# State space layers: the product with the gate behind the scan of its slot, TensorE's output product one slot later

## The chip, the cores and the metric

The kernel runs on one core of a Trainium2 chip. The metric is the device time of one execution in microseconds. A core has five engines that run side by side, each through its own instructions in their order: PE (TensorE, matrix products, with its weight loads shown as PEld), DVE (VectorE), ACT (ScalarE), POOL (GpSimd) and SP, which here only issues DMAs. They wait for one another through semaphores: a wait stops its engine, and with it all that is queued behind the wait.

## The reference, cut to what matters

The program is a chain of blocks over a batch of 8 sequences of 256 tokens with 128 features. The change lies in the second attention place, which holds four state space (Mamba) layers:

```python
for i in range(N_LAYERS):                       # 4
    xn = _layernorm(x, ln_w[i], ln_b[i])
    x = _mamba(xn, ...) + x
# _mamba
xz = einsum('bsd,ed->bse', x, in_w); x_in, z = split(xz)
xc = silu(conv(x_in) + cb)                      # 256 inner features, 4 taps
dbl = einsum('bsd,ed->bse', xc, xp_w)           # 8 for dt, 16 rows B, 16 rows C
dt = softplus(einsum(dtr, dt_w) + dt_b)
h = h * exp(dt * A) + (dt * xc) * B             # over time, 256 features x 16 states
y = sum over states of h * C
y = (y + xc * Dp) * silu(z)                     # the product with the gate
return einsum('bse,de->bsd', y, out_w)          # the output product
```

## The kernel before, in words

The 256 inner features lie as two halves (c) on 128 partitions, time along the row. A *unit* is one sequence of one layer: 4 layers x 8 sequences = 32 units, numbered 0 to 31 in this text (unit u = s + 8 l). A unit has NP = 8 *slots*, and a slot handles two of the 16 states, so that its tiles are 128 x (2 states x 2 halves x 256 steps) = 128 x 1024. `over_units` runs the slots of all units in order; per layer it writes out sequence 0, rolls sequences 1 to 4 in a loop of two pairs, and writes out 5 to 7. Each engine has its own `slot` function, called for the same slots in the same order; what it issues there is its order in the program, and semaphores couple the engines.

In slot i of a unit:
- ACT: the decays exp(dt A) of the pair i + 1 into one of two halves of a bank group (L1332, four instructions). They may start when the scan that read this half is done (`h_ready`).
- DVE: `input_term`, the product of step size, input and B for the pair i + 1 (`mam_dbu`, L1193), except for pairs 3 and 6, which POOL makes (L1267); then the scan of pair i along time (L1215), which writes `mam_state`.
- POOL: the product of the state of pair i - 1 with the rows C (`mam_state_c`, L1257), behind that pair's scan.
- PE: the sum over states, an identity matmul of `mam_state_c` of pair i - 2 that accumulates in the unit's bank (L1426, four passes for a pair). So the sum of a unit's last two pairs falls in slots 0 and 1 of the next unit.

The end of a unit lies in the next one (`last`): DVE multiplies the finished sum by the gate (`mam_y_gated`, L1200), which waits for the sum of pair 7; PE adds the residual and multiplies by the output weights (the output product, L1438 to L1444, and L1441 in the last layer alone, a second residual), which waits for `yg_ready`; ACT copies the result out of the bank in slot 4 (L1356).

Between these the engines prepare the next unit (`nxt`) and the one behind it (`after`): PE the rows for B, C and dt (L1375, L1381) in slots 0 and 1, ACT the parts of softplus in slots 1 to 3, PE their sum in slot 4 (`step_sizes`, L1411 to L1414), DVE the step sizes `mam_dt` from it, in slot 4 behind scan 4 (L1185), POOL the product of step size and input in slot 5 (L1245). The layer norm of the unit after next is taken by DVE in slot 2 (L1175, L1178), by POOL in slot 3 and by ACT and PE in slots 4 and 5; its convolution in slots 6 and 7.

No scheduler is involved: the order on each engine is the order of these functions.

Of the kernel before, what the change touches and what calls it, by code (L numbers as in the profile page):

```python
# [11 lines left out]
ALU = mybir.AluOpType  # L12
# [4 lines left out]
B, S = 8, 256  # L17
# [1068 lines left out]
def state_space_layers(K, tag, m):  # L1086
# [4 lines left out]
    NP = NS // 2  # L1091
    BY_POOL = (3, 6)
    flat = lambda a: a.rearrange("p c t -> p (c t)")
# [3 lines left out]
    y_bank = lambda q: K.ps[4 + q]  # L1097
    scratch = nc.dram_tensor(f"{tag}_bc_rows", (2 * NS, S), F32, kind="Internal").ap()
    with ExitStack() as scope:
# [12 lines left out]
        def over_units(eng, slot, tail):  # L1112
            at = lambda l, s, q: (l, s, q) if s < B else (l + 1, s - B, q) if l + 1 < L else None

            def main(l, s, q, last):
                for i in range(NP):
                    slot(i, (l, s, q), last, at(l, s + 1, 1 - q) if isinstance(s, int) else (l, s + 1, 1 - q),
                         at(l, s + 2, q) if isinstance(s, int) else (l, s + 2, q))
            for l in range(L):
                main(l, 0, 0, (l - 1, B - 1, 1) if l > 0 else None)  # L1120
                with eng.Fori(0, 2) as pair:
                    for d in (1, 2):
                        main(l, pair * 2 + d, d % 2, (l, pair * 2 + (d - 1), 1 - d % 2))
                for s in range(5, B):
                    main(l, s, s % 2, (l, s - 1, 1 - s % 2))
            for i in range(tail):
                slot(i, None, (L - 1, B - 1, 1), None, None)
# [16 lines left out]
        with nc.Block() as block:  # L1144
            @block.sync
            def _(sp):
                for u in range(L * B):
                    sp.wait_ge(rows_ready, u + 1)
                    if u:
                        for k in range(4):  # L1150
                            sp.wait_ge(loaded[k], u * 16)
                    sp.dma_start(scratch, rows[0:2 * NS, :]).then_inc(rows_out, 16)
                    sp.wait_ge(rows_out, u * 16 + 16)
                    for k in range(4):
                        if u:
                            sp.wait_ge(hc_ready, u * NP - NP + 2 * k + 2)
                        src = scratch.rearrange("(k r) t -> k (r t)", k=4)[k:k + 1, :].broadcast_to([P, 8 * S])
                        sp.dma_start(spread[:, k, :, :], src).then_inc(loaded[k], 16)

            @block.vector  # L1160
            def _(dve):
                dve.sem_inc(h_ready, 2)

                def prepare(i, nxt, after):
                    if after and i == 2:
                        l, s, q = after
                        a = s + l * B
                        xs = lambda t: xm[:, bass.ds(s * W + t * P, P)]
                        link = chain(dve, dve_s)
                        if nxt:  # L1170
                            dve.wait_ge(bias_ready, a)
                        if l > 0:
                            dve.wait_ge(done, a - B + 3)
                        for t in range(TS):
                            k = dve.bn_stats(N.bn[:, t, :], xs(t))  # L1175
                        link(k)
                        for t in range(TS):
                            k = dve.bn_aggr(N.mv[:, t, :], N.bn[:, t, :])  # L1178
                        k.then_inc(N.stats, 1)
                    if nxt and i == 4:  # L1180
                        l, s, q = nxt
                        b = s + l * B
                        dve.wait_ge(dt_sum, b + 1)
                        dve.wait_ge(relu_ready, b + 1)
                        dve.tensor_tensor(flat(dt[:, q, :, :]), K.ps[7][:, :], flat(vw[:, :, :]), ALU.add).then_inc(dt_ready, 1)  # L1185

                def input_term(u, j):
                    if j not in BY_POOL:
                        dve.wait_ge(loaded[j // 2], u * 16 + 16)
                        if not (isinstance(u, int) and u * NP + j < 4):  # L1190
                            dve.wait_ge(h_ready, u * NP + j - 1)
                        dve.wait_ge(dup_ready, u + 1)
                        dve.tensor_tensor(dbu[:, j % 4, :, :, :], both(K.ps[6][:, :].rearrange("p (c t) -> p c t", c=C)),  # L1193
                                          b_rows(j), ALU.mult).then_inc(dbu_dve, 1)

                def slot(i, now, last, nxt, after):
                    if last and i == 2:
                        l, s, q = last
                        dve.wait_ge(sum_done, (s + l * B) * NP + NP)
                        dve.tensor_tensor(flat(yg[:, :, :]), y_bank(q)[:, :], flat(zs[:, q, :, :]),  # L1200
                                          ALU.mult).then_inc(yg_ready, 1)
                    if now:
                        l, s, q = now
                        u = s + l * B
                        g = u * NP + i
                        if i + 1 < NP:
                            input_term(u, i + 1)
                        if i in BY_POOL:
                            dve.wait_ge(dbu_pool, pool_count(u, i))
                        else:  # L1210
                            dve.wait_ge(dbu_dve, dve_count(u, i))
                        if not (isinstance(u, int) and g < 4):
                            dve.wait_ge(hc_ready, g - 3)
                        dve.wait_ge(da_ready, g + 1)
                        dve.tensor_tensor_scan(flat2(h[:, i % 4, :, :, :]), decay(i), flat2(dbu[:, i % 4, :, :, :]), 0.0,  # L1215
                                               ALU.mult, ALU.add).then_inc(h_ready, 1)
                        if nxt and i + 1 == NP:
                            input_term(u + 1, 0)
                    prepare(i, nxt, after)

                before_units(prepare)
                input_term(0, 0)
                over_units(dve, slot, 3)

            @block.gpsimd
# [141 lines left out]
            def _(pe):  # L1367
# [48 lines left out]
                def slot(i, now, last, nxt, after):  # L1416
                    prepare(i, nxt, after)
                    at = lagged(i, 2, NP, now, last)
                    if at:
                        l, s, q, j = at  # L1420
                        u = s + l * B
                        if j == 0:
                            pe.wait_ge(z_ready, u + 1)
                        pe.wait_ge(hc_ready, u * NP + j + 1)
                        for n in range(2):
                            k = pe.matmul(y_bank(q)[:, :], K.ident[:, :], flat(hc[:, j % 4, n, :, :]),  # L1426
                                          start=(j == 0 and n == 0), stop=(j == NP - 1 and n == 1))
                        k.then_inc(sum_done, 1)
                        if j == 0:
                            for c in range(C):  # L1430
                                pe.matmul(y_bank(q)[:, c * S:(c + 1) * S], skip[:, l, c, :], xc[:, q, c, :],
                                          start=False, stop=False)
                    step_sizes(i, nxt)
                    if last and i == 2:
                        l, s, q = last
                        pe.wait_ge(yg_ready, s + l * B + 1)
                        for t in range(TS):
                            pe.matmul(y_bank(q)[:, t * P:(t + 1) * P], K.ident[:, :],  # L1438
                                      xm[:, bass.ds(s * W + t * P, P)], start=True, stop=False)
                            if l + 1 == L:  # L1440
                                pe.matmul(y_bank(q)[:, t * P:(t + 1) * P], K.ident[:, :],  # L1441
                                          K.x[:, bass.ds(s * W + t * P, P)], start=False, stop=False)
                            for c in range(C):
                                k = pe.matmul(y_bank(q)[:, t * P:(t + 1) * P], yg[:, c, t * P:(t + 1) * P],  # L1444
                                              f(l, "outw")[:, c * P:(c + 1) * P], start=False, stop=(c == C - 1))
                        k.then_inc(out_ps, 1)
# [3 lines left out]
                    step_sizes(i, nxt)  # L1450

                before_units(prepare_all)
                over_units(pe, slot, 3)

# [1325 lines left out]
```

## Time and profile before

| | |
|---|---|
| median of 3 runs | 2816.95 us (2815.59 to 2816.97) |
| the profiled execution | 2811.49 us, span 2809.6 us |
| mean granted TensorE clock | 0.961 of full speed |
| PE busy | 2484.8 us, 88% |
| DVE busy | 1942.2 us, 69% |
| ACT busy | 1700.1 us, 61% |
| POOL busy | 1144.5 us, 41% |

The span is the time from the first to the last instruction on the core. The shares are means over the whole program. POOL is busy 9 tenths and more of each slice only in the state space stage, from about 560 to 1434 us. There the costliest groups of the page are L1257 on POOL (256 instructions of 2360 ns), L1215 on DVE (256 of 2277 ns) and L1426 on PE (1024 passes). The page's chain of what ended last names only instructions of the last block, so it says nothing on this stage; its waits and timelines do. "Idle before" in square brackets is the time that an engine stood still ahead of an instruction, and behind the arrow is what released it. Where DVE instructions follow one another directly, a row begins some 0.08 us before the row above it ends.

### The profile page before, as it was taken

How to read it: one execution, taken by the hardware profiler on the slowest of the kernel's cores; microseconds unless marked ns; L12 is line 12 of the kernel's file. 1: busy time of each engine (PE TensorE's matmuls, PEld its weight loads, DVE VectorE, ACT ScalarE, POOL GpSimd, SP SyncE). 2: the span in 40 equal slices, each digit the busy share in tenths (PEclk: the TensorE clock that was granted, in tenths of full speed). 3: DMA queues.
4: the chain of work that ended last, by engine and by line, in shares of the span. 5: the costliest groups of instructions: out<-in, count | busy, mean ns of one | idle time of the engine just before them, and what ended most of it. 6: DMA issues, size and time to landing. Idle time of an engine off the chain costs nothing. (4 is left out here: it accounts for less than half of the span.)

```text
span 2809.6 us, 38135 instructions
## 1 busy us (share of the span) xinstructions
PE 2484.8 (88%) x11190; PEld 1409.4 (50%) x11190; DVE 1942.2 (69%) x3923; ACT 1700.1 (61%) x3566; POOL 1144.5 (41%) x919
## 2 busy tenths in 40 slices
PE   7999978499999999999978899978869998799977
PEld 4766634245555555555433344345544444555555
DVE  6888755499999999999955444356644444577754
ACT  3555522399999999999923244357754443466644
POOL 1000010299999999999930000042210001254432
PEclk9999989799999999999989999979999998999998
DMA  2000033134444444344433112000002110000000
GB/s 103 1 1 1 1 99 76 61 136 164 153 151 158 159 163 153 151 160 158 158 125 82 55 61 99 22 1 1 0 1 106 61 61 26 1 1 0 0 0 16
DMA packets 34612, 205.55 MB, mean 73 GB/s; under 512 B 4000, under 2 KB 5152, under 8 KB 13216
## 3 DMA queue, kind: packets, MB, share of 16 engines
q1 hardware_dynamic: 34464, 203.83, 20.1%
q8 instruction: 62, 1.02, 0.1%
q14 instruction: 86, 0.70, 0.1%
HBM read 201.19 MB, written 2.62 MB: 73 GB/s over the span
## 5 line engine op out<-in xcount | busy, mean ns | idle before, releaser
L1257 POOL TENSOR_TENSOR mam_state_c<-mam_state,weights_r 128x1024 f32<-128x1024 f32 x256 | 601.3, 2360 | 38.2 <-DVE mam_state L1215 37.0
L1215 DVE TENSOR_TENSOR_SCAN mam_state<-banks,mam_dbu 128x1024 f32<-128x1024 f32 x256 | 580.2, 2277 | 0.6 <-ACT banks L1332 0.6
L1426 PE MATMUL banks<-mam_state_c,identity 128*128 128x512 f32 x1024 | 479.6, 606 | 8.9 <-POOL mam_state_c L1257 8.9
L1332 ACT ACTIVATE banks<-mam_dt,mam_a_neg 128x255 f32<-128x255 f32 x1024 | 425.1, 461 | 31.9 <-DVE mam_state L1215 31.1
L1426 PEld LDWEIGHTS banks<-mam_state_c,identity 128*128 128x128 f32 x1024 | 185.4, 191 | 215.0 <-issue 181.7
L1193 DVE TENSOR_TENSOR mam_dbu<-banks,weights_r 128x1024 f32<-128x1024 f32 x192 | 227.8, 1200 | 6.8 <-ACT banks L1340 6.8
L424 ACT ACTIVATE at_probs<-banks,at_nmax 128x256 f32<-128x256 f32 x256 | 117.7, 472 | 137.8 <-DVE at_nmax L365 137.8
L2392 POOL TENSOR_TENSOR at_attention<-at_relu 128x512 f32<-128x512 f32 x128 | 131.0, 1041 | 124.4 <-ACT at_relu L2436 83.3
L896 DVE TENSOR_TENSOR m2a_hidden<-m2a_gelu,m2a_comb_spread 128x512 f32<-128x512 f32 x120 | 80.8, 690 | 116.3 <-ACT m2a_gelu L923 113.8
L896 DVE TENSOR_TENSOR m2b_hidden<-m2b_gelu,m2b_comb_spread 128x512 f32<-128x512 f32 x120 | 80.7, 690 | 116.4 <-ACT m2b_gelu L923 113.8
L1267 POOL TENSOR_TENSOR mam_dbu<-mam_dt_u,weights_r 128x1024 f32<-128x1024 f32 x64 | 151.0, 2359 | 0.0
L923 ACT ACTIVATE m2a_gelu<-banks,weights_r 128x512 f32<-128x512 f32 x128 | 85.2, 685 | 101.9 <-PE banks L943 101.8
L923 ACT ACTIVATE m2b_gelu<-banks,weights_r 128x512 f32<-128x512 f32 x128 | 85.2, 685 | 101.7 <-PE banks L943 101.7
L1762 ACT ACTIVATE at_probs<-at_scores,at_negated_max 128x160 f32<-128x160 f32 x256 | 95.0, 421 | 58.7 <-DVE at_negated_max L1601 56.0
L976 PE MATMUL banks<-m2a_hidden,weights_r 128*128 128x512 f32 x256 | 121.3, 597 | 2.2 <-DVE m2a_hidden L896 2.2
L976 PE MATMUL banks<-m2b_hidden,weights_r 128*128 128x512 f32 x256 | 121.3, 597 | 2.2 <-DVE m2b_hidden L896 2.2
L943 PE MATMUL banks<-m2a_xnt,weights_r 128*128 128x512 f32 x256 | 122.6, 602 | 0.0
L943 PE MATMUL banks<-m2b_xnt,weights_r 128*128 128x512 f32 x256 | 122.4, 601 | 0.0
L144 POOL TENSOR_SCALAR at_ln_rs<-at_ln_mv 128x2 f32<-128x2 f32 x16 | 4.4, 274 | 280.9 <-DVE at_ln_mv L346 252.2
L1400 PE MATMUL banks<-mam_xn_padded,weights_r 128*128 128x256 f32 x512 | 117.9, 383 | 0.7 <-ACT mam_xn_padded L1312 0.7
L1400 PEld LDWEIGHTS banks<-mam_xn_padded,weights_r 128*128 128x128 f32 x512 | 98.1, 192 | 28.2 <-issue 14.4
L365 DVE TENSOR_REDUCE at_nmax<-banks 128x2 f32<-128x512 f32 x128 | 82.3, 684 | 38.6 <-PE banks L468 34.5
(525 smaller groups left out, 5115.2 us busy)
## 6 DMA issues: line engine op xcount, KB each, us to landing
weights_r<-mam_bc_rows SPq DMA_DIRECT2D x128, 1024.0 KB, 4.6
m2a_comb_spread<-m2a_comb_rows SPq DMA_DIRECT2D x15, 1024.0 KB, 7.6
m2b_comb_spread<-m2b_comb_rows SPq DMA_DIRECT2D x15, 1024.0 KB, 8.2
m1a_comb_spread<-m1a_comb_rows SPq DMA_DIRECT2D x14, 512.0 KB, 7.4
m1b_comb_spread<-m1b_comb_rows SPq DMA_DIRECT2D x14, 512.0 KB, 7.1
weights_r<-in_mb SPq DMA_DIRECT2D x1, 4332.0 KB, 12.9
weights_r<-in_m SPq DMA_DIRECT2D x1, 4200.0 KB, 13.0
weights_r<-in_a SPq DMA_DIRECT2D x1, 2632.0 KB, 12.7
```

The lines of the kernel that those rows point to most:

```text
L896: dve.tensor_tensor(hid[:, g % 3, c, :], gelu[:, g % 2, c, :], weights, ALU.mult).then_inc(hid_ready, 1)
L923: act.activation(gelu[:, g % 2, c, :], h_bank(g, c)[:, :], ACT.Gelu, bias=b1[:, 2 * e + c:2 * e + c + 1]).then_inc(gelu_ready, 1)
L943: pe.matmul(h_bank(g, c)[:, :], w1[:, e * 256 + c * P:e * 256 + (c + 1) * P], R.xnt[:, p % 2, :], start=True, stop=True).then_inc(h_ps, 1)
L976: i = pe.matmul(y[:, :], w2[:, (2 * e + c) * P:(2 * e + c + 1) * P], hid[:, g % 3, c, :], start=False, stop=(e == E - 1 and c == 1))
L1193: dve.tensor_tensor(dbu[:, j % 4, :, :, :], both(K.ps[6][:, :].rearrange("p (c t) -> p c t", c=C)), b_rows(j), ALU.mult).then_inc(dbu_dve, 1)
L1215: dve.tensor_tensor_scan(flat2(h[:, i % 4, :, :, :]), decay(i), flat2(dbu[:, i % 4, :, :, :]), 0.0, ALU.mult, ALU.add).then_inc(h_ready, 1)
L1257: pool.tensor_tensor(hc[:, j % 4, :, :, :], h[:, j % 4, :, :, :], c_rows(j), ALU.mult).then_inc(hc_ready, 1)
L1267: pool.tensor_tensor(dbu[:, (i + 2) % 4, :, :, :], both(du[:, q, :, :]), b_rows(i + 2), ALU.mult).then_inc(dbu_pool, 1)
L1332: i = act.activation(decay(j)[:, o + 1:o + S], dt[:, q, c, 1:S], ACT.Exp, scale=aneg[:, l, k:k + 1])
L1400: k = pe.matmul(K.ps[7][:, c * S:(c + 1) * S], f(l, "taps")[:, t * 256 + c * P:t * 256 + (c + 1) * P], xpad[:, q, t:t + S], start=(t == 0) ...
L1426: k = pe.matmul(y_bank(q)[:, :], K.ident[:, :], flat(hc[:, j % 4, n, :, :]), start=(j == 0 and n == 0), stop=(j == NP - 1 and n == 1))
L2392: pool.tensor_tensor(at[:, i % 4, :, :], rel[:, i % 4, :, :], rel[:, i % 4, :, :], ALU.mult).then_inc(at_ready, 1)
```

## The change

On DVE, in the slot with i == 2, the product of the unit before with its gate is issued behind the scan of the slot and no longer ahead of it. On PE, the output product of the unit before is issued in slot 3, behind the sum over pair 1, and no longer in slot 2, behind the sum over pair 0. The tail of PE's slots behind the last unit is one slot longer for that.

```diff
 def slot(i, now, last, nxt, after):          # DVE
-    if last and i == 2:
-        l, s, q = last
-        dve.wait_ge(sum_done, (s + l * B) * NP + NP)
-        dve.tensor_tensor(flat(yg[:, :, :]), y_bank(q)[:, :], flat(zs[:, q, :, :]),
-                          ALU.mult).then_inc(yg_ready, 1)
     if now:
...
         if nxt and i + 1 == NP:
             input_term(u + 1, 0)
+    if last and i == 2:
+        l, s, q = last
+        dve.wait_ge(sum_done, (s + l * B) * NP + NP)
+        dve.tensor_tensor(flat(yg[:, :, :]), y_bank(q)[:, :], flat(zs[:, q, :, :]),
+                          ALU.mult).then_inc(yg_ready, 1)
     prepare(i, nxt, after)
...
     step_sizes(i, nxt)                       # PE
-    if last and i == 2:
+    if last and i == 3:
         l, s, q = last
         pe.wait_ge(yg_ready, s + l * B + 1)
...
-over_units(pe, slot, 3)
+over_units(pe, slot, 4)
```

PE's order before, in a unit outside the rolled loop, from the sum over pair 7 of the unit before and pair 0 (the first row, `x4`) to the step sizes of slot 4:

```order
L1426 MATMUL banks<-mam_state_c,identity 128x512 x4
L1431 MATMUL banks<-mam_conv,mam_skip_diagonal 128x256 x2
L1438 MATMUL banks<-mam_xm,identity 128x128
L1444 MATMUL banks<-weights_r,mam_y_gated 128x128 x2
L1438 MATMUL banks<-mam_xm,identity 128x128
L1444 MATMUL banks<-weights_r,mam_y_gated 128x128 x2
L1426 MATMUL banks<-mam_state_c,identity 128x512 x4
L1411 MATMUL banks<-mam_dt_exp,identity 128x512
L1412 MATMUL banks<-mam_dt_abs,identity 128x512
L1414 MATMUL banks<-mam_dt_ln,identity 128x512
```

The same place now:

```order
L1426 MATMUL banks<-mam_state_c,identity 128x512 x4
L1431 MATMUL banks<-mam_conv,mam_skip_diagonal 128x256 x2
L1426 MATMUL banks<-mam_state_c,identity 128x512 x2
L1438 MATMUL banks<-mam_xm,identity 128x128
L1444 MATMUL banks<-weights_r,mam_y_gated 128x128 x2
L1438 MATMUL banks<-mam_xm,identity 128x128
L1444 MATMUL banks<-weights_r,mam_y_gated 128x128 x2
L1426 MATMUL banks<-mam_state_c,identity 128x512 x2
L1411 MATMUL banks<-mam_dt_exp,identity 128x512
L1412 MATMUL banks<-mam_dt_abs,identity 128x512
L1414 MATMUL banks<-mam_dt_ln,identity 128x512
```

The output product stood ahead of the sums over pairs 1 and 2, and stands between them now.

DVE's order before in the same unit, from the input term of slot 1 to scan 2:

```order
L1193 TENSOR_TENSOR mam_dbu<-banks,weights_r 128x1024
L1211 REGISTER_ALU
L1213 REGISTER_ALU
L1214 REGISTER_ALU
L1215 SCALAR_TENSOR_TENSOR mam_state<-banks,mam_dbu 128x1024
L1200 TENSOR_TENSOR mam_y_gated<-banks,mam_gate 128x512
L1211 REGISTER_ALU
L1214 REGISTER_ALU
L1215 SCALAR_TENSOR_TENSOR mam_state<-banks,mam_dbu 128x1024
```

And now (L1206 to L1210 are the lines 1211 to 1215 of before, L1217 is the line 1200):

```order
L1193 TENSOR_TENSOR mam_dbu<-banks,weights_r 128x1024
L1206 REGISTER_ALU
L1208 REGISTER_ALU
L1209 REGISTER_ALU
L1210 SCALAR_TENSOR_TENSOR mam_state<-banks,mam_dbu 128x1024
L1206 REGISTER_ALU
L1209 REGISTER_ALU
L1210 SCALAR_TENSOR_TENSOR mam_state<-banks,mam_dbu 128x1024
L1217 TENSOR_TENSOR mam_y_gated<-banks,mam_gate 128x512
```

The gate product went from between scans 1 and 2 to behind scan 2. The orders of ACT, POOL and SP are the same in both kernels.

## Rows read from the trace of the kernel before

**Rows 1.** Busy time by stretch: first unit, units 1 to 9, the last layer's periods.

```profile
core 0: us, PE busy (x) PEld busy (x) DVE busy (x) ACT busy (x) POOL busy (x), PEclk, DMA share, GB/s
562.46:589.40 26.94, 22.97 (x60) 12.09 (x60) 25.57 (x20) 23.98 (x49) 24.11 (x15) 0.83 0.28 102
589.40:832.53 243.13, 232.75 (x757) 125.91 (x756) 235.49 (x181) 229.04 (x459) 232.76 (x136) 1.00 0.43 158
1237.81:1401.77 163.96, 155.76 (x515) 84.51 (x514) 156.98 (x118) 151.33 (x302) 154.96 (x87) 1.00 0.41 158
```

**Rows 2.** Waits of the state space stage: who waited for whom, us in total, times, longest.

```profile
POOL mam_state_c L1257 <- DVE mam_state L1215: 37.0, 33, 10.9
DVE mam_y_gated L1200 <- PE banks L1426: 29.6, 31, 5.2
DVE mam_dt L1185 <- PE banks L1414: 3.3, 7, 1.3
```

**Rows 3.** Timeline of DVE, unit 14: start us, us, engine line op, tiles, count [idle before].

```profile
947.00 0.69 DVE L1200 TENSOR_TENSOR mam_y_gated<-banks,mam_gate 128x512 f32<-128x512 f32 x1 [0.81 <-PE banks L1426]
954.88 2.28 DVE L1215 TENSOR_TENSOR_SCAN mam_state<-banks,mam_dbu 128x1024 f32<-128x1024 f32 x1
957.08 0.68 DVE L1185 TENSOR_TENSOR mam_dt<-banks,mam_dt_relu 128x512 f32<-128x512 f32 x1
974.03 0.69 DVE L1200 TENSOR_TENSOR mam_y_gated<-banks,mam_gate 128x512 f32<-128x512 f32 x1 [0.81 <-PE banks L1426]
```

**Rows 4.** Timeline of PE, unit 14.

```profile
949.38 0.38 PE L1438 MATMUL banks<-mam_xm,identity 128*128 128x128 f32 x2
950.72 3.75 PE L1426 MATMUL banks<-mam_state_c,identity 128*128 128x512 f32 x8
954.30 1.02 PE L1411 MATMUL banks<-mam_dt_exp,identity 128*128 128x512 f32 x2
956.01 1.02 PE L1414 MATMUL banks<-mam_dt_ln,identity 128*128 128x512 f32 x2
```

**Rows 5.** Timeline of PE's weight loads, unit 14.

```profile
952.48 0.30 PEld L1426 LDWEIGHTS banks<-mam_state_c,identity 128*128 128x128 f32 x2 [0.71 <-POOL mam_state_c L1257]
```

**Rows 6.** Timeline of POOL, unit 14 and the start of 15.

```profile
943.04 2.35 POOL L1257 TENSOR_TENSOR mam_state_c<-mam_state,weights_r 128x1024 f32<-128x1024 f32 x1 [0.51 <-DVE mam_state L1215]
947.68 4.75 POOL L1257 TENSOR_TENSOR mam_state_c<-mam_state,weights_r 128x1024 f32<-128x1024 f32 x2
961.08 1.28 POOL L1245 TENSOR_TENSOR mam_dt_u<-mam_dt,mam_conv 128x512 f32<-128x512 f32 x1
970.07 2.35 POOL L1257 TENSOR_TENSOR mam_state_c<-mam_state,weights_r 128x1024 f32<-128x1024 f32 x1 [0.76 <-DVE mam_state L1215]
```

**Rows 7.** Timeline of ACT, unit 14: the copy of the output product.

```profile
956.47 0.36 ACT L1356 ACTIVATE mam_xm<-banks 128x256 f32<-128x256 f32 x1
```

**Rows 8.** Timeline of DVE, unit 0, which has no product with the gate.

```profile
578.85 0.69 DVE L1185 TENSOR_TENSOR mam_dt<-banks,mam_dt_relu 128x512 f32<-128x512 f32 x1 [1.33 <-PE banks L1414]
```

**Rows 9.** Timeline of DVE and PE, unit 1, inside the loop.

```profile
605.88 0.66 DVE L1185 TENSOR_TENSOR mam_dt<-banks,mam_dt_relu 128x512 f32<-128x512 f32 x1
604.71 1.02 PE L1414 MATMUL banks<-mam_dt_ln,identity 128*128 128x512 f32 x2
```

**Rows 10.** Timeline of PE, POOL and DVE, unit 27, last layer.

```profile
1301.25 0.39 PE L1438 MATMUL banks<-mam_xm,identity 128*128 x2
1303.04 3.60 PE L1426 MATMUL banks<-mam_state_c,identity 128*128 128x512 f32 x8
1306.47 1.02 PE L1411 MATMUL banks<-mam_dt_exp,identity 128*128 128x512 f32 x2
1308.19 1.02 PE L1414 MATMUL banks<-mam_dt_ln,identity 128*128 128x512 f32 x2
1299.44 2.37 POOL L1257 TENSOR_TENSOR mam_state_c<-mam_state,weights_r 128x1024 f32<-128x1024 f32 x1
1309.25 0.69 DVE L1185 TENSOR_TENSOR mam_dt<-banks,mam_dt_relu 128x512 f32<-128x512 f32 x1 [0.21 <-PE banks L1414]
```

## The prediction

> **What bounds the kernel now.** I read the windows by stretch first, since the change touches only the state space stage, which runs from about 560 to 1434 us of the span. It is 32 units (4 layers, 8 sequences) of 8 slots. In units 1 to 9 every engine is nearly full: of 243.13 us DVE is busy 235.49, POOL 232.76, PE 232.75, ACT 229.04, at a TensorE clock of 1.00 [rows 1]. Shares of busy time can't name the bound here: four engines within 3% of each other are a ring of waits, and the ring's length is what counts. 243.13 / 9 is 27.01 us for a unit; unit 0 takes 26.94, a unit of the last layer 163.96 / 6 = 27.33.
>
> The waits are read second. DVE waits 29.6 us for PE's sum ahead of its product with the gate (L1200), 31 times, of which 5.2 us are the last product of the stage; the 30 others, one in each of units 1 to 30, are (29.6 - 5.2) / 30 = 0.81 us each. DVE also waits 3.3 us in 7 cases for PE at the step sizes (L1185), and POOL waits for DVE's scan, once 10.9 us at the start and then once in a unit [rows 2].
>
> The timelines of unit 14 are read third, to see which of these waits is the bound. I number the products with C (POOL, L1257) and the scans 0 to 7 by slot.
> - POOL starts product 0 at 943.04, product 1 at 947.68, and that of the next unit at 970.07, after 0.76 us of waiting for scan 0. Its two products of 4.75 us end at 952.43, so that product 1 ends at about 950.03 and product 2 at 952.43 [rows 6].
> - PE's sum over product 2 starts at 952.48, released by POOL [rows 5], the step sizes' three matmuls follow at 954.30, the last begins at 956.01 and ends at 957.03 [rows 4].
> - DVE starts the step sizes at 957.08, 0.05 us after PE's end. No idle time is shown there, for its scan of 954.88 is only just done [rows 3]. So DVE arrives in the same instant as PE's result. From there to POOL's next product 0 it is 970.07 - 957.08 = 12.99 us of scans and input products on DVE.
>
> That is a closed ring: POOL product 0, 1, 2 (to 952.43), PE's sum and step sizes (4.65 us), DVE (12.99 us), POOL again: 14.04 + 12.99 = 27.03 us, as long as the unit (974.03 - 947.00 = 27.03, [rows 3]). The wait ahead of the gate product lies on another ring of just this length. Take it away and DVE comes 0.81 us sooner to L1185, where it waits for PE. Unit 0 shows it: there is no gate product and no wait in front of one, and DVE waits 1.33 us at L1185 [rows 8]; the unit is still 26.94 us long. So the wait that the edit on DVE removes is worth about 0.1 us in a unit at most.
>
> **The change part by part.** No instruction is added or removed. DVE: the gate product goes behind scan 2. Scan 2 can start at once, 0.81 us earlier, and the product starts when it ends, at 947.00 - 0.81 + 2.2 = 948.4, done at 949.1; PE's sum was ready at 947.0, so it waits for nothing. By itself it is worth between 0 and -0.1 us a unit, by the ring above; beside the second edit nothing is left of it.
>
> PE: the output product goes behind the sum over product 1. This is where I see a cost. Before, PE took the output product at 949.38, was through at 950.72 (1.34 us), did the sum over product 1, four passes, until about 952.43, and was free exactly when product 2 came at 952.43 [rows 4, 6]. The output product filled the time in which POOL was still at product 1. Now, in the same frame:
> - PE is free at 949.38 and the next in its order is the sum over product 1, ready at 950.03. With the 0.05 us of a release [rows 5] it starts at 950.08: a hole of 0.70 us.
> - A sum behind a wait takes 954.30 - 952.48 = 1.82 us: PE is free at 951.90. The gate product (949.1) is there.
> - Output product 1.34 us: 953.24.
> - Sum over product 2, no wait any more. Eight passes of this kind without a wait take 1306.47 - 1303.04 = 3.43 us [rows 10], so 1.71: 954.95.
> - Step sizes 957.03 - 954.30 = 2.73, and 0.05 to the release: DVE starts L1185 at 957.73 in place of 957.08, +0.65 us. It wanted to start it at 956.27, so it waits about 1.5 us there.
>
> Everything behind hangs on that: scans 5 to 7, the next scan 0, POOL's product 0. The ring is 27.03 + 0.65 = 27.68 us. POOL's own work between stays covered: it is in an unbroken row from product 0 on, and now idles 0.76 + 0.65 us. ACT's copy of the output product (956.47, [rows 7]) finds it at 953.4 in place of 950.9, 3 us ahead; ACT's other work follows the scans and moves with them.
>
> Units in the rolled loop (sequences 1 to 4) have a margin: in unit 1 PE ends at 605.73 and DVE starts at 605.88 [rows 9], 0.15 in place of 0.05, so 0.10 us of the delay is absorbed and with the roundings the cost is 0.57. In the last layer the output product has four passes more, 1303.04 - 1301.25 = 1.79 us, and PE is busy without a hole up to the step sizes, for which DVE waits 0.21 us [rows 10]. Now product 1 ends at 1299.44 + 2.37 = 1301.81, and 0.05 + 1.82 + 1.79 + 1.71 + 2.74 + 0.05 later is 1309.97, against 1309.25: +0.72, and in units whose POOL waits 0.09 us more +0.81.
>
> The sum over the units with an output product and step sizes (1 to 30): layers 0 to 2 inside the loop 12 x 0.57 = 6.8, the other 12 x 0.65 = 7.8, the last layer 6 x 0.76 = 4.6. Unit 0 has no output product. Unit 31 has no step sizes, and its gate product is not among the waits [rows 2]: 0. After it the order is as before. Sum +19.2 us. The profiled execution took 2811.49 us (span 2809.6), so 2830.7 for one like it; the median of the runs, which stands 5.5 us above it, becomes 2816.95 + 19.2 = 2836.2.
>
> What the trace doesn't show is a hole in that place. Bounds: if the ring had a slack that I don't see, up to the 0.15 us of rows 9 in each unit, 30 x 0.5 = +15; if each unit lost the whole hole and the release besides, 0.8 us, +24. A gain is excluded as long as PE's result at L1185 is the later one. I take the middle since three lengths fit: the ring from rows is 27.03, the unit is 27.03, and four short passes more in the last layer made the unit 0.31 us longer.
>
> **The rivals.**
> *Faster: POOL becomes the bound.* If DVE's arrival at L1185 were only by chance as late as PE's, the wait of 0.81 us goes, POOL's 0.76 us ahead of product 0 goes with it, and a unit is 27.03 - 0.76 = 26.27: 30 x 0.76 = -23, 2794 us. For it: the regular wait on the busiest engine. Against it: unit 0 [rows 8] and the last layer [rows 10]. It decides as soon as PE's step sizes end before 956.3 in this frame. The Trainium skill (Perfetto Trace Analysis, "Identifying the Most-Contended Engine" and "Optimization Strategy") says to take the engine with the highest occupancy first and to remove what causes its repeating gaps. By that rule DVE's gap is the one to remove and the time would be this rival's. The trace does not bear it out: DVE is at 97%, yet a unit without the gap was no shorter.
>
> *No change.* PE's delay is absorbed: it would need PE to be early at the start of the unit by enough that step sizes aren't late, which the order of waiting for product 1 forbids. Then only the 0.0 to 0.1 us a unit of the first edit is left: 2814 to 2817.
>
> *Slower by more.* The later step sizes push POOL's product of step size and input and ACT's copy into the bank, and with them the next decays; a second wait of 0.3 to 0.5 us a unit: +10 to +15 on top, 2846 to 2851. Against it: POOL came to that product at 961.08 [rows 6], 3.3 us behind the step sizes' end (957.08 + 0.68, [rows 3]), and had no idle time there.
>
> *That the change doesn't do what it says* is excluded by the order of the instructions: both moves are there in every unit, and ACT, POOL and SP are unchanged.
>
> **How the numbers follow.** Forecast 0.83, POOL bound 0.06, no change 0.06, slower by more 0.05. The time is 2836. The forecast's own spread is 2832 to 2841; with a run's scatter and a part of the hole absorbed I take 2828 to 2842. What a measurement can tell from no change is 0.2%, 5.6 us. Slower by over 0.2% (above 2822.6) holds the forecast and the last rival, 0.87; faster 0.06; within 0.2% 0.07.
>
> **What would show it.** Right: the wait at the gate product is gone from the table of waits, in its place DVE waits at L1185 for L1414 some 1.4 to 1.5 us in each of 30 units (42 to 46 us in total, from 3.3); POOL waits for scan 0 about 1.4 us a unit; PE shows a hole of 0.7 us ahead of the sum over product 1; units of 27.6 to 27.7 us, 28.1 in the last layer; the stretch behind the stage as long as before. Wrong: units under 27.0 us, or L1185 without a wait, or a unit as long as 27.7 with the wait somewhere else.

## The result: slower by 0.8%, at the step sizes

The changed kernel takes 2837.8 us (median of 4, 2833.64 to 2839.38), against 2816.39 us (median of 4) for the kernel before, timed with it: a ratio of 1.0078, 95% interval 1.0065 to 1.009. The forecast was 2836.2. The profiled execution took 2839.38 us, span 2837.6.

The windows of the changed kernel, cut at the first scan of the stage and at its last gate product, with the columns of [rows 1]; the same cuts of before gave 562.46, 867.14 and 1380.00 us:

```profile
0.00:563.64 563.64, 474.50 (x2590) 304.33 (x2590) 385.79 (x1144) 250.01 (x750) 48.36 (x94) 0.93 0.14 43
563.64:1450.42 886.78, 825.35 (x2646) 440.75 (x2646) 832.41 (x629) 798.59 (x1604) 822.16 (x471) 0.99 0.40 148
1450.42:2837.60 1387.18, 1202.91 (x5954) 672.95 (x5954) 722.94 (x2152) 651.63 (x1213) 272.85 (x354) 0.94 0.10 36
```

The stage went from 867.14 to 886.78 us, +19.6, and every engine's busy time in it is within 3 us of before: nothing got more work, the engines stand still longer. The other 8.4 us of the difference between the two spans lie outside the stage, 1.2 ahead of it and 7.2 behind, in code that is the same in both kernels. Behind the stage DVE is busy 722.94 us against 722.91, while the same 5954 matmuls keep PE busy for 1202.91 us against 1192.68, at a granted clock of 0.94 against 0.95. The only-PE experiment below, whose stage is as long as this one's, took 1384.7 us for that last stretch, others 1379.6 to 1382.6, and its five executions alone lie 7.9 us apart (2831.09 to 2838.97). So these 8.4 us are put down to scatter between executions, and 19.6 us to the change.

The waits of the changed kernel in the same stage (us in total, times, longest), which answer to [rows 2]:

```profile
POOL mam_state_c L1257 <- DVE mam_state L1210: 58.6, 34, 10.9
DVE mam_dt L1185 <- PE banks L1414: 48.2, 31, 2.6
DVE mam_y_gated L1217 <- PE banks L1426: 5.2, 1, 5.2
```

The wait ahead of the gate product is gone but for the last one, 24.4 us less. At the step sizes DVE waits 48.2 us in place of 3.3, and in all of the 31 units that have them in place of 7. POOL waits 21.6 us longer: its wait for scan 0, once in a unit, is 1.4 to 1.5 us in most units and 1.8 to 1.9 in the last layer, where before it was 0.7 to 0.8 and 1.0 to 1.15.

The timeline of PE in unit 14, for [rows 4]:

```profile
957.79 1.03 PE L1431 MATMUL banks<-mam_conv,mam_skip_diagonal 128*128 128x256 f32 x4
959.35 1.99 PE L1426 MATMUL banks<-mam_state_c,identity 128*128 128x512 f32 x4 [0.54 <-POOL mam_state_c L1257]
961.17 0.38 PE L1438 MATMUL banks<-mam_xm,identity 128*128 128x128 f32 x2
962.51 1.88 PE L1426 MATMUL banks<-mam_state_c,identity 128*128 128x512 f32 x4
964.23 1.02 PE L1411 MATMUL banks<-mam_dt_exp,identity 128*128 128x512 f32 x2
965.95 1.02 PE L1414 MATMUL banks<-mam_dt_ln,identity 128*128 128x512 f32 x2
```

Here is the hole. The skip product starts at 957.79 and four passes of it take 0.87 us before the next can start (so it was before), that is 958.66; the sum over product 1 starts at 959.35, released by POOL: 0.69 us. (The brackets of the row say 0.54, since the profile draws a matmul's end some 0.15 us later than the next one can start; the 0.69 are taken from the starts, as the forecast's 0.70 were.) Then 1.82 us, the output product from 961.17 to 962.51, the sum over product 2 from 962.51 without a wait, the step sizes from 964.23, ended at 966.97.

DVE and POOL in the same unit, for [rows 3, 6]:

```profile
957.56 0.67 DVE L1217 TENSOR_TENSOR mam_y_gated<-banks,mam_gate 128x512 f32<-128x512 f32 x1
967.01 0.69 DVE L1185 TENSOR_TENSOR mam_dt<-banks,mam_dt_relu 128x512 f32<-128x512 f32 x1 [1.49 <-PE banks L1414]
```

```profile
952.32 2.35 POOL L1257 TENSOR_TENSOR mam_state_c<-mam_state,weights_r 128x1024 f32<-128x1024 f32 x1 [1.25 <-DVE mam_state L1210]
956.94 4.67 POOL L1257 TENSOR_TENSOR mam_state_c<-mam_state,weights_r 128x1024 f32<-128x1024 f32 x2
980.00 2.35 POOL L1257 TENSOR_TENSOR mam_state_c<-mam_state,weights_r 128x1024 f32<-128x1024 f32 x1 [1.51 <-DVE mam_state L1210]
```

POOL's product 1 ends at 956.94 + 2.35 = 959.29, and PE's sum starts 0.06 us later. The ring, which now passes through product 1 and no longer through product 2, is POOL's 952.32 to DVE's 967.01, 14.69 us (14.04 before), and from there to POOL's 980.00, 12.99 us as before: 27.68. DVE has 1.49 us of idle time in front of the step sizes.

In the last layer, PE and DVE of unit 27, for [rows 10]:

```profile
1319.62 1.98 PE L1426 MATMUL banks<-mam_state_c,identity 128*128 128x512 f32 x4 [0.45 <-POOL mam_state_c L1257]
1323.23 1.88 PE L1426 MATMUL banks<-mam_state_c,identity 128*128 128x512 f32 x4
1326.67 1.02 PE L1414 MATMUL banks<-mam_dt_ln,identity 128*128 128x512 f32 x2
```

```profile
1327.72 0.69 DVE L1185 TENSOR_TENSOR mam_dt<-banks,mam_dt_relu 128x512 f32<-128x512 f32 x1 [1.86 <-PE banks L1414]
```

From the first scan of unit 1 to that of unit 25 the changed kernel needs 27.65 us a unit, in the last layer 28.08 (before: 27.02 and 27.33).

### The profile page after: what moved, and what is told of

The parts are those of the page before. It is cut to its first block and busy times, and to the rows that moved or that the text cites. A ratio compares the mean times of both kernels' runs of the same rounds, so it can differ in the third digit from the quotient of the medians.

```text
span 2837.6 us, 38135 instructions
## 1 busy us (share of the span) xinstructions
PE 2502.8 (88%) x11190; PEld 1418.0 (50%) x11190; DVE 1941.1 (68%) x3923; ACT 1700.2 (60%) x3566; POOL 1143.4 (40%) x919
## 5 line engine op out<-in xcount | busy, mean ns | idle before, releaser
L1210 DVE TENSOR_TENSOR_SCAN mam_state<-banks,mam_dbu 128x1024 f32<-128x1024 f32 x256 | 577.2, 2276 | 0.6 <-ACT banks L1332 0.6
L1426 PE MATMUL banks<-mam_state_c,identity 128*128 128x512 f32 x1024 | 483.4, 604 | 26.4 <-POOL mam_state_c L1257 26.4
L1332 ACT ACTIVATE banks<-mam_dt,mam_a_neg 128x255 f32<-128x255 f32 x1024 | 425.0, 461 | 70.1 <-DVE mam_state L1210 69.2
```

The costliest lines, as they stand in the source:

```text
L1332: i = act.activation(decay(j)[:, o + 1:o + S], dt[:, q, c, 1:S], ACT.Exp, scale=aneg[:, l, k:k + 1])
```

## The experiments

Six kernels were run, all with five rounds against the kernel before. The first four of them shared its runs (median 2813.69 us), and so did the last two (2815.89). The period of a unit is taken between first scans, over units 1 to 24 and over the six periods of the last layer; the windows cut there are shown for the ones whose verdict rests on them.

### Only the edit on DVE

```diff
-                    if last and i == 3:      # PE, output product
+                    if last and i == 2:
...
-over_units(pe, slot, 4)
+over_units(pe, slot, 3)
```
(against the changed kernel)

> Only the edit on DVE: the gate product behind scan 2, PE's output product in slot 2 as before. Theory (ring over POOL's products 0 to 2, PE's sum and step sizes, DVE's scans): the wait of 0.81 us moves from the gate product to the step sizes (L1185), a unit stays at 26.9 to 27.0 us, the last layer at 27.3; ratio to before 0.999 to 1.000. Rival (the gate product's wait is the bound, POOL is next): units of 26.3 us, 23 us less, ratio 0.992.

Measured: 2812.6 us, ratio 0.9997 (0.9988 to 1.0006), no difference that can be told. Its waits and its windows:

```profile
DVE mam_dt L1185 <- PE banks L1414: 26.4, 31, 1.8
DVE mam_y_gated L1217 <- PE banks L1426: 5.2, 1, 5.2
```

```profile
589.48:1235.62 646.14, 619.57 (x2017) 335.92 (x2016) 627.71 (x482) 610.95 (x1224) 620.01 (x361) 1.00 0.44 157
1235.62:1399.59 163.97, 155.59 (x515) 84.59 (x514) 156.31 (x118) 151.36 (x302) 154.97 (x87) 1.00 0.43 158
```

24.4 us of waiting at the gate product became 23.1 us more at the step sizes (26.4 in place of 3.3). A unit is 646.14 / 24 = 26.92, 0.10 less than before, and 27.33 in the last layer. The whole stage is 2.3 us shorter in the trace, less than the times can tell. POOL as the next bound, 26.3 us, did not show itself. Taken by the starts of L1185, a unit is 26.88 us inside the rolled loop and 26.96 outside it, against 27.01 and 27.02 before: that is the length of the ring over the step sizes when nothing else holds the unit.

### Only the edit on PE

```diff
-                    if last and i == 2:      # PE, output product
+                    if last and i == 3:
...
-over_units(pe, slot, 3)
+over_units(pe, slot, 4)
```
(against the kernel before)

> Only the edit on PE: the output product in slot 3, the gate product ahead of scan 2 as before. Theory: the whole cost is here; units of 27.6 to 27.7 us, 28.1 in the last layer, +19 to +20 us, ratio 1.007; DVE waits about 0.8 us at the gate product and about 0.6 to 0.7 us at the step sizes. Rival (the cost comes from the two edits together, DVE running early and then being late): less than half of it, ratio under 1.0035.

Measured: 2831.29 us, ratio 1.0065 (1.0051 to 1.0079). Its waits and windows:

```profile
DVE mam_y_gated L1200 <- PE banks L1426: 24.6, 30, 0.8
DVE mam_dt L1185 <- PE banks L1414: 20.5, 31, 1.7
```

```profile
592.66:1256.17 663.51, 625.04 (x2017) 335.75 (x2016) 630.28 (x481) 610.87 (x1224) 621.73 (x361) 1.00 0.42 154
1256.17:1424.63 168.46, 157.20 (x515) 84.08 (x514) 156.95 (x117) 151.35 (x302) 154.54 (x87) 1.00 0.41 151
```

663.51 / 24 = 27.65 and 168.46 / 6 = 28.08, to the hundredth what the changed kernel has. The whole cost is PE's edit. DVE's two waits sum to 45.1 us here, and its one wait to 48.2 in the changed kernel (30 x 0.08 = 2.4 us of the difference is the overlap of rows, which a second wait in a unit takes away). So the ring decides how long DVE stands still, and the order of its own work only at which of the two places. That DVE's edit costs nothing beside PE's is seen in the stage, 886.75 us here and 886.78 with both edits.

### Half of the output product back in slot 2

```diff
-                    if last and i == 3:
+                    if last and i in (2, 3):
                         l, s, q = last
-                        pe.wait_ge(yg_ready, s + l * B + 1)
-                        for t in range(TS):
+                        if i == 2:
+                            pe.wait_ge(yg_ready, s + l * B + 1)
+                        for t in (i - 2,):
...
-                        k.then_inc(out_ps, 1)
+                        if i == 3:
+                            k.then_inc(out_ps, 1)
```
(against the changed kernel)

> The changed kernel, with the first half of the output product (128 of the 256 steps) in slot 2 and only the second half in slot 3. PE's work is the same. Theory (the cost is the hole of 0.70 us ahead of the sum over product 1): the first half, 0.67 us, fills the hole, the step sizes are late by 0.06 us in place of 0.65; units of 27.0 to 27.1, ratio to before 0.999 to 1.001. Rival (the cost is that PE work stands between the sums, whatever its place before): half of the cost stays, +10 us, ratio 1.0035.

Measured: 2813.2 us, ratio 0.9991 (0.9975 to 1.0008); 26.98 us a unit, 27.33 in the last layer. PE's timeline in unit 14:

```profile
949.34 0.38 PE L1439 MATMUL banks<-mam_xm,identity 128*128 128x128 f32 x2
950.04 1.98 PE L1426 MATMUL banks<-mam_state_c,identity 128*128 128x512 f32 x4
951.86 0.38 PE L1439 MATMUL banks<-mam_xm,identity 128*128 128x128 f32 x2
952.53 1.88 PE L1426 MATMUL banks<-mam_state_c,identity 128*128 128x512 f32 x4
955.97 1.02 PE L1414 MATMUL banks<-mam_dt_ln,identity 128*128 128x512 f32 x2
```

The first half (949.34 to 950.04) fills the hole while product 1 is made, the second (951.86 to 952.53) fills the time up to product 2 and overruns it by a little: POOL ends product 2 at about 952.3, and PE's sum starts at 952.53. That little is what is left of the cost: 26.98 us a unit against 26.92 with DVE's edit alone, 0.06 us, as expected. In the last layer nothing is left (27.33 in both). So it is the hole that costs, and not that PE's work stands between the sums.

### Step sizes ahead of the sum over product 2

Three kernels carry this edit: the changed kernel, the kernel before, and the DVE edit alone.

```diff
 def slot(i, now, last, nxt, after):          # PE
     prepare(i, nxt, after)
+    step_sizes(i, nxt)
     at = lagged(i, 2, NP, now, last)
...
-    step_sizes(i, nxt)
     if last and i == 3:                      # 2 in the other two
```

On the changed kernel:

> The changed kernel, with PE's step size matmuls of slot 4 ahead of the sum over product 2, not behind it. Theory: the ring over product 2 is cut; PE reaches the step sizes at 953.24 in the frame of unit 14 and ends them at about 956.0, where DVE wants them at 956.3; the hole ahead of product 1 stays but nothing waits for it. Then POOL (26.3 us a unit) or ACT's chain bounds: units of 26.3 to 26.5, 16 to 22 us under before, ratio 0.992 to 0.994. Rival (the later output product costs by itself, through ACT's copy or the sum): still slower than before.

Measured: 2792.54 us, ratio 0.9927 (0.9913 to 0.9941). Waits of the stage, windows, and DVE at unit 14:

```profile
POOL mam_state_c L1257 <- DVE mam_state L1210: 14.1, 9, 10.9
DVE mam_dt L1185 <- PE banks L1414: 0.6, 1, 0.6
```

```profile
589.46:1221.45 631.99, 621.92 (x2016) 335.57 (x2015) 628.96 (x481) 607.09 (x1226) 620.38 (x362) 1.00 0.44 161
1221.45:1379.74 158.29, 156.84 (x517) 84.30 (x515) 156.62 (x117) 150.70 (x303) 155.29 (x88) 1.00 0.45 165
```

```profile
935.48 4.47 DVE L1210 TENSOR_TENSOR_SCAN mam_state<-banks,mam_dbu 128x1024 f32<-128x1024 f32 x2 [0.27 <-ACT banks L1332]
947.74 0.66 DVE L1185 TENSOR_TENSOR mam_dt<-banks,mam_dt_relu 128x512 f32<-128x512 f32 x1
```

With the output product still in slot 3, a unit is 26.33 us, 26.38 in the last layer. Neither POOL nor DVE waits for long: DVE is busy 628.96 of 631.99 us. Between 590 and 1380 us DVE waits 0.9 us for ACT's decays and 0.6 us once for PE, and POOL waits 1.5 us for DVE's scans. Each waits for less than 0.1 us a unit, and these runs don't tell which of the two sets the 26.33. A cost of the later output product by itself does not show.

On the kernel before, both of the change's edits left out:

> The kernel before, with PE's step size matmuls of slot 4 ahead of the sum over product 2. Both edits of the change are left out. Theory (two rings of 27.0 us, one over the gate product, one over the step sizes): cutting the second alone gives nothing, units of 27.0; only the last layer may go from 27.33 to 27.0, -2 us; ratio 0.999 to 1.000, and the gate product still waits 0.8 us. Rival (only the ring over the step sizes is real, the gate product's wait follows it): units of 26.3 to 26.5, ratio 0.993.

Measured: 2812.11 us, ratio 0.9989 (0.998 to 0.9998). Its wait at the gate product:

```profile
DVE mam_y_gated L1200 <- PE banks L1427: 30.0, 31, 5.1
```

```profile
589.72:1238.73 649.01, 619.30 (x2018) 337.73 (x2016) 627.82 (x482) 611.74 (x1226) 621.87 (x362) 1.00 0.43 158
1238.73:1400.11 161.38, 154.75 (x513) 84.27 (x513) 156.30 (x117) 151.44 (x302) 154.08 (x87) 1.00 0.44 159
```

27.04 us a unit, as before, and 161.38 / 6 = 26.90 in the last layer, which the step sizes had bound at 27.33 (the last of the six, unit 30, which has no layer norm to prepare, is 26.36, the others 27.0). The ring over the gate product is real too: cut the other and this one holds the unit at 27.0. The prediction didn't say what this ring runs over. The trace of before has, from unit 14:

```profile
943.51 0.36 ACT L1284 ACTIVATE mam_bc_dt_rows<-banks 40x256 f32<-40x256 f32 x1
943.92 1.12 PE L1381 MATMUL banks<-mam_bc_dt_rows,weights_r 9*128 9x256 f32 x4 [0.32 <-ACT mam_bc_dt_rows L1284]
963.31 1.67 ACT L1332 ACTIVATE banks<-mam_dt,mam_a_neg 128x255 f32<-128x255 f32 x4 [0.27 <-DVE mam_state L1215]
```

From the gate product at 947.00 DVE works without a wait to scan 6, whose end releases ACT at 963.31. ACT is then in an unbroken row of decays, convolution, gate and decays up to its rows (L1284, at 943.51 and again 27.02 us later), which release PE's rows (L1381, at 943.92 and again at 970.95). Behind those PE takes the sum over pair 7, and DVE's next gate product follows at 974.03. That is 16.31 + 7.64 + 3.08 = 27.03 us over DVE, ACT and PE, and POOL is not on it. With the step sizes first the same three parts measure 16.29, 7.64 and 3.07, together 27.00 us.

On the DVE edit alone, so that both rings are cut and the output product is in slot 2:

> The gate product behind scan 2 (the change's edit on DVE), PE's output product in slot 2 as before, and the step size matmuls of slot 4 ahead of the sum over product 2. Theory: both rings are cut, units of 26.3 to 26.5, 16 to 22 us under before, ratio 0.992 to 0.994, much as with the output product in slot 3. Rival: ACT's chain from POOL's product of step size and input to the decays binds at 26.8 or more, ratio over 0.997.

Measured: 2791.52 us, ratio 0.9914 (0.9901 to 0.9928).

```profile
589.91:1221.98 632.07, 616.48 (x2016) 337.56 (x2015) 628.89 (x481) 607.70 (x1226) 620.17 (x362) 1.00 0.44 162
1221.98:1380.08 158.10, 155.82 (x517) 84.79 (x515) 156.81 (x117) 150.92 (x303) 155.21 (x88) 1.00 0.45 165
```

26.34 and 26.35 us: as with the output product in slot 3, and the two can't be told apart. Both beat the kernel before and the changed kernel. By the ratios the DVE edit is worth 1 us alone (not told from none), step sizes first 3 us alone, and the two together 24 us.

## Why the prediction was right

- *The bound: a closed ring of 27.03 us over POOL's products, PE's step sizes and DVE's scans, beside another of the same length over the gate product.* Shown, each by cutting the other: DVE's edit alone leaves 26.92, step sizes first alone leaves 27.04, both together 26.33. The two are not quite equal, though. By itself the ring over the step sizes is 26.88 us in the rolled loop, 26.96 outside it and 27.33 in the last layer, and the one over the gate product is 27.00. In layers 0 to 2 the latter is the longer one, by 0.04 to 0.12 us, in the last layer the former.
- *The edit on DVE is worth at most 0.1 us a unit.* It measured 27.02 - 26.92 = 0.10 by itself. The prediction took this from unit 0, which has no gate product and was 0.07 us shorter than the others. That was weaker evidence than it sounds, since unit 0 has no output product either and ran at a granted clock of 0.83 [rows 1]; the experiment shows what unit 0 only suggested.
- *The edit on PE opens a hole of 0.70 us ahead of the sum over product 1.* It is 0.69 us in unit 14, and filling it with half of the output product takes the cost away.
- *Step sizes 0.65 us later, 0.57 in the rolled loop, 0.72 to 0.81 in the last layer.* In unit 14 the way from POOL's product 0 to the step sizes grew from 14.04 to 14.69. Between the starts of L1185 a unit grew by 0.59 us in the rolled loop, by 0.67 in the other units of layers 0 to 2 and by 0.75 in the last layer. Against DVE's edit alone, where the same ring is by itself, it grew by 0.72, 0.73 and 0.75: the hole and the release count almost in full in every unit, and the cost comes out smaller in layers 0 to 2 because the unit of before, with the gate product ahead of scan 2, was 0.13 and 0.06 us longer than this ring by itself. The prediction saw this only in the loop, as a margin between PE's end and DVE's start at L1185.
- *Sum +19.2 us.* The stage grew by 19.6. The median moved by 21.4 us, with an interval of 18 to 25 us (the ratio's bounds times 2816): the trace's 19.6 lies inside it. That the forecast of 2836.2 lies 1.6 us from the median of 2837.8 is closer than four runs between 2833.64 and 2839.38 can confirm, and is in part luck; the growth of the stage is the comparison that counts.
- *DVE waits 1.4 to 1.5 us at L1185, 42 to 46 us in total.* It was 1.40 to 1.51 in units 1 to 24, but 1.85 to 1.95 in units 25 to 29 and 2.58 in unit 30. The table has 48.2 us, or 46.9 without the 1.3 of unit 0, which was there before: a little above the range. The range had been given without the last layer's share; the sum of the time had it. POOL's wait for scan 0, forecast at about 1.4 us, was 1.4 to 1.5 in units 1 to 24.
- *The stretch behind the stage as long as before.* This sign did not come: the stretch was 7.2 us longer, with the instructions of before and at the slightly lower clock given above.
- *Rival "POOL becomes the bound", 26.27 us a unit.* It did not come with this change, though it is nearly what is left when both rings are cut (26.33), where DVE is as full as POOL. The rule of the Trainium skill (Perfetto Trace Analysis, "Optimization Strategy"), to look for what blocks the repeating gaps of the most occupied engine, did not gain anything by itself here: with DVE's edit alone the gap was removed, and the same time stood at the next place where DVE waits. Only with both rings cut did removing DVE's gaps pay, 24 us. The question that decides is whether the engine, once freed, arrives anywhere sooner.
- *Rivals "no change" and "slower by more".* Neither occurred; POOL's and ACT's waits grew only where they wait for DVE's scans (ACT's from 31.1 to 69.2 us), which come later with the step sizes. Of the chances, 0.83 + 0.05 for slower is 0.88, where the prediction has 0.87 for it and one hundredth more than its rival for no change; nothing hangs on it.

## What to carry to other kernels

Where several engines are nearly full, as here at 94 to 97% of units 1 to 9, follow a repeating wait to the next place where the same engine waits for another, and compare when both arrive: if that second meeting is already tight, removing the first wait moves it and does no more. Two rings of nearly equal length must be cut together, and an experiment that cuts one and finds nothing has not shown that it doesn't matter. Before moving work out of the way on an in-order engine, ask what it was covering: the output product cost nothing in the gap while POOL finished the operand of PE's sum, and 0.65 us a unit, on average over 30 units, once it stood behind that sum.

## What was not expected of the hardware

The same last stretch of the program, with the same instructions, took 1380.00 us in the trace of before and 1387.18 in that of after, at a mean granted TensorE clock of 0.95 and 0.94. PE was busy for 10.2 us more with the same number of matmuls, and DVE for as long as before. The state space stage, by contrast, at 0.99 to 1.00, came out within 0.03 us in two kernels with the same bound (886.78 and, with PE's edit alone, 886.75). A difference of under 1% is better read from the stage that changed than from two spans.
